# The first quarter of the output weights is loaded into the still unused x2T, at the start of the q-projection block

## What is computed

```python
def feature_map(x):
    norm = jnp.sqrt(jnp.sum(x * x, axis=-1, keepdims=True))
    return x / jnp.maximum(norm, 1e-12)

# attention part, X = layernorm(x), D = 2048, rot_dim = D // 2
QKV = jnp.einsum('bsd,ed->bse', X, W_in) + b_in
Q, K, V = jnp.split(QKV, 3, axis=-1)
Q = rope(Q, rot_dim)
K = rope(K, rot_dim)
A = jnp.sum(feature_map(K) * V, axis=-2)
Y = A[:, None, :] * Q
Y = jnp.einsum('bsd,ed->bse', Y, W_out) + b_out
x = x + (Y + X)

# expert part, xf = layernorm(x), E = 8, TOPK = 2
logits = jnp.einsum('td,ed->te', xf, gate_w)
# gates: softmax over the two largest logits of each token, 0 elsewhere
y = jnp.einsum('td,edo->eto', xf, expert_w) + expert_b[:, None, :]
out = jnp.einsum('te,eto->to', gates, y)
x = x + out
```

## Time and profile before

| what | value |
|---|---|
| time, median of 2 runs | 2035.3 us (2033.92 to 2036.67) |
| the profiled execution, its own time | 2038.65 us |
| its span on the slowest core (core 3) | 2037.1 us |
| spans of the 8 cores | 2022.9 to 2037.1 us |
| TensorE (PE) busy | 1681.1 us (83%) |
| VectorE (DVE) busy | 639.3 us (31%) |
| ScalarE busy | 59.3 us (3%) |
| GpSimd (POOL) busy | 69.8 us (3%) |
| mean granted TensorE clock, core 3 | 0.914 |

### The profile page before, as it was taken

How to read it: one execution, slowest core, us unless ns; L and a number is a source line. 1 busy time by engine, 2 the same in 40 slices (tenths; PEclk the granted TensorE clock), 3 DMA queues, 4 the chain that set the end, 5 groups by cost and what they waited for, 6 DMA issues and landing times.

```text
span 2037.1 us, 19626 instructions; the slowest of 8 cores (2022.9 to 2037.1 us)
## 1 busy us (share of the span) xinstructions
PE 1681.1 (83%) x7905; PEld 771.2 (38%) x7905; DVE 639.3 (31%) x1069; ACT 59.3 (3%) x62; POOL 69.8 (3%) x71
## 2 busy tenths in 40 slices
PE   1499589349958959833965999999999999999998
PEld 0244233124423424321433444444444444444442
DVE  3421143742204342276155222222222222222224
ACT  1300000130000000000000000000000000000000
POOL 1000000000000000000000000000000000000000
PEclk9999799659978979956986999999999999999997
DMA  9332652723265334327520544445554445554444
GB/s 173 96 45 39 93 86 70 134 93 47 37 93 100 56 57 77 59 69 174 79 46 1 84 77 67 66 80 83 83 83 68 65 74 83 83 83 74 67 67 165
DMA packets 132368, 161.80 MB, mean 79 GB/s; under 512 B 6577, under 2 KB 127409, under 8 KB 128185
## 3 DMA queue, kind: packets, MB, share of 16 engines
q0 software_dynamic: 118544, 120.66, 38.5%
q1 hardware_dynamic: 13738, 39.90, 6.1%
HBM read 272.79 MB, written 8.41 MB: 138 GB/s over the span
## 4 chain that ended last, share of the span: by engine, by line
PE 48%; DVE 3%; DMA 1%; issue 1%; DVEq 1%; ACT 0%; ACTq 0%; SPq 0%; POOLq 0%
PE ps_m L973 44%; PE ps_m L738 4%; DMA x_scr<-x_all 1%; DVE st L256 1%; PE ps_tr L324 1%; DVE xln_scr L304 1%; DVE x L716 0%; DVE x L926 0%; DVE x L711 0%; DMA bb_scr<-biases 0%; DVE x2T L345 0%; DVEq L258 0%; PE ps_l L795 0%; DVEq L254 0%; ACT L283 0%
## 5 line engine op out<-in xcount | busy, mean ns | idle before, releaser
L973 PE MATMUL ps_m<-wbuf,x2T 128*128 128x512 bf16 x4096 | 887.1, 380 | 0.2 <-issue 0.2
L458 PE MATMUL ps_m<-wbuf,xlnT 128*128 128x512 bf16 x2560 | 577.2, 390 | 76.9 <-DMA wbuf<-w_vT 45.2
L973 PEld LDWEIGHTS ps_m<-wbuf,x2T 128*128 128x128 bf16 x4096 | 401.4, 98 | 485.6 <-issue 4.2
L986 DVE SCALAR_TENSOR_TENSOR x<-ps_m,gates,x 128x512 f32<-128x512 f32 x256 | 192.3, 751 | 695.4 <-PE ps_m L973 695.4
L458 PEld LDWEIGHTS ps_m<-wbuf,xlnT 128*128 128x128 bf16 x2560 | 255.4, 100 | 398.4 <-issue 112.1
L324 PE MATMUL ps_tr<-ident_bf,xln_scr 128*128 128x128 bf16 x384 | 45.1, 308 | 150.3 <-DVE xln_scr L304 150.3
L738 PE MATMUL ps_m<-wbuf,qT 128*128 128x512 bf16 x512 | 116.2, 391 | 34.6 <-DVE x L751 31.7
L470 DVE TENSOR_TENSOR v_sb<-ps_m,bb_scr 128x512 bf16<-128x512 f32 x64 | 43.7, 690 | 209.3 <-PE ps_m L458 209.3
L470 DVE TENSOR_TENSOR k_sb<-ps_m,bb_scr 128x512 bf16<-128x512 f32 x64 | 44.3, 692 | 182.1 <-PE ps_m L458 182.1
L324 PEld LDWEIGHTS ps_tr<-ident_bf,xln_scr 128*128 128x128 bf16 x384 | 38.4, 141 | 156.8 <-issue 155.8
L738 PEld LDWEIGHTS ps_m<-wbuf,qT 128*128 128x128 bf16 x512 | 51.1, 100 | 99.0 <-issue 42.3
(11 more groups left out here) (72 smaller groups left out, 334.4 us busy)
## 6 DMA issues: line engine op xcount, KB each, us to landing
wbuf<-e_w POOLq DMA_DIRECT2D x32, 2048.0 KB, 14.9
x_scr<-x_all SPq DMA_DIRECT2D x24, 1024.0 KB, 6.6
wbuf<-w_kT POOLq DMA_DIRECT2D x8, 2048.0 KB, 19.3
wbuf<-w_vT POOLq DMA_DIRECT2D x8, 2048.0 KB, 19.9
wbuf<-w_qT POOLq DMA_DIRECT2D x4, 2048.0 KB, 16.9
wbuf<-w_oT POOLq DMA_DIRECT2D x4, 2048.0 KB, 15.8
y<-x SPq DMA_DIRECT2D x8, 1024.0 KB, 6.1
bb_scr<-biases POOLq DMA_DIRECT2D x6, 512.0 KB, 6.9
```

What stands on the lines that cost most here:

```text
L458: mm = te.matmul(ps[:, :], self.xlnT[:, dc, t * 128:(t + 1) * 128], self.wbuf[q % 2][:, dc, :], start=(dc == 0), stop=(dc == ND - 1))
L973: mm = te.matmul(ps[:, :], self.x2T[:, dc, t * 128:(t + 1) * 128], self.wbuf[si % 2][:, dc, :], start=(dc == 0), stop=(dc == ND - 1))
L986: sv.inc(v.scalar_tensor_tensor(out=self.x1[:, t, q * OCW:(q + 1) * OCW], in0=ps[:, :], scalar=self.gates[:, t, e_i:e_i + 1], in1=self.x1[ ...
```

## The change

The load of output weights for quarter 0 goes into the first 512 columns of x2T, with a semaphore of its own, sow. POOL issues it as the first entry of the q-projection block, ahead of the bias of q; the load into wbuf0 behind the RoPE of q is gone. x2T is therefore allocated ahead of q_sb, and released last. In `phase_oproj` the matmuls of quarter 0 wait for sow and read x2T as their right operand; quarters 1 to 3 read wbuf as before. Quarter 0 of the output projection no longer sets `free["wbuf0"]`, so what POOL waits for ahead of the load of quarter 2 into wbuf0 is the last reader in the q projection.

```diff
@@ build()
         esQ = contextlib.ExitStack()
+        esX2 = contextlib.ExitStack()
+        self.x2T = esX2.enter_context(
+            nc.sbuf_tensor("x2T", [128, ND, S2], BF16, side="right"))
         self.q_sb = esQ.enter_context(
             nc.sbuf_tensor("q_sb", [128, NTO, D], BF16, side="right"))
...
             self._mk_psum(ps_es)
+            @blk.gpsimd
+            def _(g):
+                g.dma_start(
+                    out=self.x2T[:, :, 0:OCW],
+                    in_=self.w_oT.rearrange("(dc p) o -> p dc o", p=128)
+                    [:, :, 0:OCW]).then_inc(self.sow.h, 16)
+                self.sow.n += 16
             self.phase_proj(blk, 0, "q")
...
             self.phase_rope_q_transpose(blk)
-            self._emit_wdma(blk, "o", 0)
...
@@ phase_oproj()
         for q in range(NQ):
-            swp = self.swp[q % 2]
-            w_done = self._get_wdma(blk, "o", q)
+            if q == 0:
+                swp, w_done = self.sow, 16
+                rhs_of = lambda dc: self.x2T[:, dc, 0:OCW]
+            else:
+                swp = self.swp[q % 2]
+                w_done = self._get_wdma(blk, "o", q)
+                rhs_of = lambda dc, q=q: self.wbuf[q % 2][:, dc, :]
...
-                            self.wbuf[q % 2][:, dc, :],
+                            rhs_of(dc),
...
-            self.free[f"wbuf{q % 2}"] = (sp, sp.n)
+            if q != 0:
+                self.free[f"wbuf{q % 2}"] = (sp, sp.n)
```

More of the change, by code:

```diff
@@ L118, in build @@
         self.sgt = Sem(e(nc.semaphore("sgt")))
+        self.sow = Sem(e(nc.semaphore("sow")))
         self.sg = Sem(e(nc.semaphore("sg")))
@@ L183, in build @@
             nc.sbuf_tensor("x1", [128, NTO, D], F32, side="right"))
-        esX2 = contextlib.ExitStack()
-        self.x2T = esX2.enter_context(
-            nc.sbuf_tensor("x2T", [128, ND, S2], BF16, side="right"))
         with contextlib.ExitStack() as ps_es, nc.Block() as blk:
@@ L198, in build @@
             self.phase_biasmix(blk)
-        esX2.close()
-        esQT.close()
         self.phase_store()
         esX1.close()
+        esQT.close()
+        esX2.close()
         es0.close()
@@ L733, in _ @@
                 @blk.tensor
-                def _(te, q=q, t=t, ps=ps, w_done=w_done, swp=swp, pnm=pnm):
+                def _(te, q=q, t=t, ps=ps, w_done=w_done, swp=swp, pnm=pnm,
+                      rhs_of=rhs_of):
                     te.wait_ge(swp.h, w_done)
```

## The result

The changed kernel is slower by 1.4%: the ratio is 1.0139 with an interval of 1.0092 to 1.0186. The medians over all executions are 2085.69 us (11 executions, 2059.03 to 2331.31) against 2038.24 us (10 executions, 2033.92 to 2217.83). The other six of the changed kernel took 2059.03, 2060.61, 2060.68, 2060.72, 2061.27 and 2085.69 us, with a median of 2060.7. The profiled execution took 2061.98 us.

The account below looks back on a forecast made before the run. The slowest core's TensorE was taken as the bound: expert matmuls almost without idling, 34.6 us idle in the output projection. Added costs of 15.2 + 6 = 21.2 us took the 2035.3 median to 2057 us, range 2041 to 2064.

Parts of the forecast that it names:

- What the change takes away: Old load of output weights for quarter 0, 67 us to spare before use: removing it there gives nothing back.
- The first term: Start of q-projection block: bias lands late behind the moved 2 MB load; 13.2 us stall plus 2.0 restart, 15.2 us.
- The bound below: q-projection start: moved load alone takes 15.7 us, so the bias lands at 760.5 at the earliest; stall 6.7 us.
- The queue goes in turn: POOL's queue at the q-projection start: transfers finish one after another, so the bias behind 2 MB lands at 767.0.
- The formula of the Trainium skill: q-projection start: 2.0 us plus bytes over 436 GB/s, so 2 MB take 6.8 us and the stall is close to nothing.
- The second term: Output-projection start: quarter 2's load, issued early beside the x transfers, slows tiles 4 and 5; 6 us, bounds 0 and 9.0.
- the 9.5 of the bound: Output projection: upper bound with all four later x transfers at 9.5 us each, making the block 9.0 us longer.
- How the numbers follow: Whole kernel: range 2041 to 2064 us for 8 in 10, chance 0.96 of staying within 2% of before.
- Side by side: POOL's queue shares time among transfers: bias early, quarter 1 lands 2 to 3 us late; about 2046 us, chance 0.17.
- The x transfers not suffering: Output projection: x transfers lose little to the extra load, only the q-projection cost of 15.2 remains; 2050.5 us, chance 0.14.
- No change: Both places: moved load through in under 8 us, second load gone before the x transfers; 2035 to 2038 us, chance 0.05.
- the lasting low clock: q projection: the new stall leaves TensorE at the lower clock; over 2% slower, from 2077 us on, chance 0.03.

Follow-up runs that it names:

- The run with both terms mended: Changed kernel with the moved load issued behind quarter 1 of the q weights and output-weight quarter 2 held as in the kernel before: 2037.6 us against 2036.8.
- the first experiment: Changed kernel with the q bias issued first, the moved load second, quarter 1 of the q weights third: 2049.6 us, 1.0068 of the kernel before.
- the first two experiments: Changed kernel with the moved load put second in POOL's queue, behind the q bias (2049.6 us), or third, behind quarter 1 of the q weights (2044.2 us).
- the second comparison: The same changed kernel, unaltered, measured again beside the kernel before: 2061.3 against 2036.1 us, ratio 1.0121.
- the first four experiments: Changed kernel with moved load second or third in queue, quarter 2 of output weights held, or third and held: 2049.6, 2044.2, 2053.4, 2037.6 us.

## Why the prediction was right in its mechanism and wrong in its number

**What the change takes away.** Right: nobody waited for the moved load, and taking it away from its old place gave nothing. The run with both terms mended shows that, with a ratio of 1.0006 (0.9994 to 1.0017).

**The first term, forecast 15.2 us, measured 17.7 (15.5 of stall and 2.2 of restart).** The bias was to land at 767.0 and landed at 769.1; the stall was to be 13.2, and TensorE's restart came 15.5 later, counted from the block's start (25.3 against 9.85 us); the restart at the lower clock was to cost 2.0 and cost 2.2. The argument from the same bytes in the other order held within 2.1 us. The bound below was poor: I took 15.7 us for a 2 MB load, from one issued in the middle of a block, and at the block's start, with the bias and 2 MB more behind it, it took 21.9 (23.1 in the first experiment). SP's transfers for aT and the rope tables, or loads of the neighbouring core, may have a share in it; no run tells. That TensorE would not wait for quarter 1 held: its list of waits has no w_qT.

**The queue goes in turn.** Right, and shown by the first two experiments: the bias took 7.8 us with 4 MB behind it and 23.3 with 2 MB ahead of it. The formula of the Trainium skill (DMA: Bandwidth & Descriptors, section "Anatomy of one DMA — SWDGE (gpsimd) path"), with the 2 MB that are written, would have made the term vanish; the trace does not agree with it: 21.9 us, not 6.8.

**The second term, forecast 6, measured 6.5 (7.3 in the second comparison).** Right, with its mechanism: the transfers of tiles 4 and 5 took 9.6 and 8.8 us, and the term went when the load was held. That the size came so close is in part luck. I had quarter 2 landing at 954.7, 40.7 us into the block; it landed 48.9 us into it, so tile 7 was not undisturbed. Against that the transfers of tiles 6 and 7, beside the load to their ends, took 7.5 and 7.2 us and not the 9.5 of the bound.

**The sum.** 21.2 forecast, 24.2 in the traces. The measured ratios, 1.0139 and 1.0121, have intervals that hold the forecast of 2057 / 2035.3 = 1.0107 (1.0092 to 1.0186, and 1.0100 to 1.0142), so in size it was short by 3 us, 2.5 of them in the first term.

**What failed** is the step "How the numbers follow", and in it the term of "some 3 us, the distance of the profiled execution from the median", the only allowance for how far one execution lies from another. The measured median over all executions, 2085.69, lies outside the range of 2041 to 2064, though the middle of the executions that the ratio rests on, 2060.7, lies inside it. The term of 3 us stood for a spread that I had read from three executions. The runs showed 2033.9 to 2217.8 us before the change and 2059.0 to 2331.3 after it. Executions like the one at 2085.69 come without the change too: the kernel before took 2064.7, 2073.9, 2076.0 and 2087.5 us in the comparison of the first four experiments. The range was put around the cost of the change alone. Whether the change has a part in how far single executions lie above the rest was not tried and stays open. The term of the sum that was mis-sized most is the landing of the bias, 767.0 forecast and 769.1 measured, which made 15.2 us of the first term where the trace has 17.7; that alone would have left the time inside the range.

**The rivals.** Side by side (0.17): refuted by the bias landing at 7.8 and 23.3 us. The x transfers not suffering (0.14): refuted in both directions. No change (0.05) and the lasting low clock (0.03): neither came; the clock was back at 1.00 after about 4 us.

## What to carry to other kernels

A load that is issued early costs nothing only if nothing behind it in its queue is wanted soon: ask of each moved transfer which small, urgent one now stands behind it, and put the small one first. When a buffer comes free early, the queue will use it early; look at what else moves bytes at that time, and hold the load if nobody waits for it. The same reading found 42 us in one line of code, because a queue entry that waits for a late event holds back the weights behind it.

## What was not expected of the hardware

On the slowest cores, bytes ahead of a transfer in a queue don't cost evenly: 10.1 us for the first MB, 5.4 for the second, 11.7 for the next two together. A pair of loads in the kernel before has the same shape, with 20.4 us for the first and 10.4 more for the second. But these are all cores that reach the block later than their neighbour (0 and 1, 2 and 3, and so on). Over all cores the bias lands after, in us:

| MB ahead | the later core of each pair | the earlier core of each pair |
|---|---|---|
| 0 | 7.3 to 8.5 | 5.9 to 6.1 |
| 1 | 16.7 to 18.2 | 11.2 to 12.4 |
| 2 | 23.3 to 24.4 | 18.5 to 20.9 |
| 4 | 34.8 to 35.7 | 30.5 to 32.8 |

On the earlier cores the first MB adds some 6 us and the second some 8, so the dear first MB is a matter of which core of the pair it is, and not of the queue alone. No run here shows what the neighbour does to it.

The cores of the changed kernel fall into two groups within each neighbouring pair, and so do their stalls for the bias, as here on cores 0 and 1:

```profile
PE ps_m L465 <- DVE q_sb L477: 10.9, 1, 10.9
```

```profile
PE ps_m L465 <- DVE q_sb L477: 16.2, 1, 16.2
```

The pairs 2 and 3, 4 and 5, 6 and 7 have 16.9 and 13.1, 15.7 and 12.8, 13.3 and 16.1 us. In each pair the core that reached the block earlier stalled less, and its span is shorter by 14.4, 13.6, 12.8 and 10.4 us. The stalls make 5.3, 3.8, 2.9 and 2.8 us of that; in the kernel before the two cores of a pair already differed by 5.5, 6.7, 7.1 and 7.0 us. That one core of a pair is served while the other waits would fit, but no experiment was made on it.
